# A Mamba layer and a LoRA feed-forward on eight cores: ScalarE's evacuations pulled forward, and the feed-forward in blocks of 512 tokens with streamed W2

## The reference, cut

```python
def _L0_attn_ref(x, ...):
    xz = jnp.einsum('bld,ed->ble', x, W_in)
    xc, z = jnp.split(xz, 2, axis=-1)          # xc: causal conv over 4 tokens, then silu
    ...
    xp = jnp.einsum('bld,ed->ble', xc, W_x)
    delta = jax.nn.softplus(xp[..., -1:] * w_dt + b_dt)
    dA = jnp.exp(delta[..., None] * A)
    dBx = (delta * xc)[..., None] * B_in[:, :, None, :]
    # h = dA_t * h + dBx_t ; y_t = sum_n h * C_t      (scan over the tokens)
    y = ys.transpose(1, 0, 2) + D_param * xc
    y = y * jax.nn.silu(z)
    return jnp.einsum('ble,de->bld', y, W_out)

def _L0_ffn_ref(x, W1, b1, W2, b2, scale):
    lt = jax.lax.dynamic_slice_in_dim(x, LORA_TOKEN_INDEX, LORA_DIM, axis=1)
    even = lt[:, ::2, :]; odd = lt[:, 1::2, :]
    m1 = (even[:, :4, :, None] * odd[:, :4, None, :]).reshape(Bx, Hx, Dx)
    m2 = (even[:, 4:, :, None] * odd[:, 4:, None, :]).reshape(Bx, Dx, Hx)
    h = x @ W1.T + scale * einsum(x, m1) + b1
    h = jax.nn.gelu(h, approximate=False)
    return h @ W2.T + scale * einsum(h, m2) + b2

x = _layernorm(x + _L0_attn_ref(x, ...))
x = _layernorm(x + _L0_ffn_ref(x, ...))
```

## Time and profile before

| | us |
|---|---|
| median of two runs | 8405.77 |
| profiled execution | 8392.8 |
| its slowest core (core 1), first to last instruction | 8391.2 |
| fastest core's span | 8322.1 |
| PE busy | 3725.1 (44%) |
| VectorE busy | 4821.4 (57%) |
| ScalarE busy | 3446.1 (41%) |
| GpSimd busy | 391.0 (5%) |

### The profile page before, as it was taken

The page is one execution under the profiler, slowest core; times in us unless marked ns, Lnnn a source line. Parts: engine busy times, 40 slices in busy tenths (PEclk is TensorE's granted clock), DMA queues, the critical chain, the costliest instruction groups (busy, mean ns, idle before and its releaser), DMA issues.

```text
span 8391.2 us, 72518 instructions; the slowest of 8 cores (8322.1 to 8391.2 us)
## 1 busy us (share of the span) xinstructions
PE 3725.1 (44%) x21344; PEld 2186.9 (26%) x21344; DVE 4821.4 (57%) x5521; ACT 3446.1 (41%) x8573; POOL 391.0 (5%) x522
## 2 busy tenths in 40 slices
PE   4446424234241433424243242433420078887888
PEld 2123313122130312313132131312210034444444
DVE  1000679797887979779797877969778500100010
ACT  4443545454454545445353454535434122222222
POOL 0010000000000000000000000000001000000000
PEclk9999657667675766766566675656765589888888
DMA  3676322223232222322223232222320310010000
GB/s 84 112 129 157 105 60 88 64 82 101 58 99 55 93 78 70 106 61 88 61 83 99 59 100 59 88 72 80 103 53 3 61 53 16 23 11 13 16 20 14
DMA packets 521966, 582.43 MB, mean 69 GB/s; under 512 B 413311, under 2 KB 413311, under 8 KB 482672
## 3 DMA queue, kind: packets, MB, share of 16 engines
q1 hardware_dynamic: 491408, 482.62, 18.9%
q0 software_dynamic: 30176, 95.17, 6.4%
HBM read 581.51 MB, written 71.84 MB: 78 GB/s over the span
## 4 chain that ended last, share of the span: by engine, by line
DVE 34%; DVEq 21%; PE 19%; DMA 6%; issue 5%; ACT 4%; another core or an unknown queue 1%; POOLq 1%; ACTq 0%; POOL 0%; SPq 0%
DVE hc L789 13%; DVEq L794 13%; PE ps_h L965 6%; PE ps_oB L993 6%; DMA wout_r<-woutT_scr 4%; DVE dbx L763 4%; DVE hc L807 4%; DVE hc L802 4%; DVEq L806 3%; DVEq L770 3%; PE ps_wo L380 2%; DVE hc L809 2%; DVE gtmp L815 1%; PE ps_h L968 1%; DVE hc L811 1%
## 5 line engine op out<-in xcount | busy, mean ns | idle before, releaser
L789 DVE TENSOR_TENSOR_SCAN hc<-dA,dbx 128x2048 bf16<-128x2048 f16 x512 | 2238.5, 4414 | 20.7 <-issue 2.3
L706 ACT ACTIVATE dA<-delta,a_sb 128x256 f16<-128x256 f32 x4096 | 1666.8, 494 | 431.9 <-DVE hc L789 428.0
L584 PE MATMUL ps_xz<-xT,w1s_r 128*128 128x256 bf16 x8192 | 1129.5, 305 | 522.5 <-ACT xc L659 391.9
L763 DVE TENSOR_TENSOR dbx<-vv,brep 128x2048 bf16<-128x2048 bf16 x512 | 607.4, 1228 | 867.6 <-ACT dA L706 651.2
L584 PEld LDWEIGHTS ps_xz<-xT,w1s_r 128*128 128x128 bf16 x8192 | 871.0, 109 | 751.4 <-issue 548.5
L600 PE MATMUL ps_xz<-xT,win_r 128*128 128x256 bf16 x2048 | 422.9, 389 | 1207.3 <-ACT zsil L667 1015.9
L380 PE MATMUL ps_wo<-wout_r,ybuf 128*128 128x512 bf16 x1024 | 332.3, 464 | 1322.8 <-DVE ybuf L819 1117.9
L802 DVE TENSOR_TENSOR hc<-hc,crep 128x2048 bf16<-128x2048 bf16 x512 | 612.8, 1238 | 20.1 <-issue 1.5
L600 PEld LDWEIGHTS ps_xz<-xT,win_r 128*128 128x128 bf16 x2048 | 263.6, 134 | 1361.1 <-issue 1262.8
L965 PE MATMUL ps_h<-y1T,w1t_sb 128*128 128x256 bf16 x4096 | 581.3, 289 | 18.3 <-DVE su_sb L1060 16.9
L706 ACT ACT_TABLE_LOAD x150 | 192.4, 1283 | 882.9 <-DVE hc L789 882.7
(11 more groups left out here) (116 smaller groups left out, 3990.3 us busy)
## 6 DMA issues: line engine op xcount, KB each, us to landing
w1s_r<-win1s_scr SPq DMA_DIRECT2D x256, 1024.0 KB, 5.0
win_r<-winT_scr SPq DMA_DIRECT2D x256, 256.0 KB, 2.9
wout_r<-woutT_scr SPq DMA_DIRECT2D x256, 256.0 KB, 2.6
win1s_scr<-p_stage SPq DMA_DIRECT2D x64, 256.0 KB, 2.3
brep<-bc_scr POOLq DMA_DIRECT2D x16, 1024.0 KB, 9.1
crep<-bc_scr POOLq DMA_DIRECT2D x16, 1024.0 KB, 13.4
out<-outsb SPq DMA_DIRECT2D x32, 512.0 KB, 3.2
p_wrow<-W_in POOLq DMA_DIRECT2D x48, 256.0 KB, 4.8
```

The costliest lines, as they stand in the source:

```text
L584: jx = t.matmul(pst[:], w1s_ring[jj % 2][:, (k4 * NKD + kt) * P:(k4 * NKD + kt + 1) * P], xT[par][:, kt * TE + 1 + k4:kt * TE + 1 + k4 + T ...
L706: jx = s.activation(da_t[:, n8 * T:(n8 + 1) * T], delta[dt % 8][:], AF.Exp, scale=a_sb[:, dt * NST + n:dt * NST + n + 1])
L763: jx = v.tensor_tensor(dbx[(jh0 + nh) % 4][:].rearrange("p (n t) -> p n t", n=8), vv[par][:, dt * T:(dt + 1) * T].unsqueeze(1) .broadcast_ ...
L789: jx = v.tensor_tensor_scan(hc[:, nh * 8 * T:(nh + 1) * 8 * T], dA[(jh0 + nh) % 4][:], dbx[(jh0 + nh) % 4][:], 0.0, OP.mult, OP.add)
```

## The change

Stage A: `prep_evac` for the next chunk runs in steps 4 to 10 (5, 5, 5, 5, 4, 4 and 4 of them) instead of 4 to 15, and `prep_xpev` at step 12 instead of behind step 15.

Stage B: blocks of TB = 512 tokens, 8 instead of 16. `w2t_sb` is gone; W2 comes in slabs of 128 x 1024 through four buffers `w2_r`, issued by SP, and is read twice a block (two passes of two token tiles each; four PSUM tiles are filled side by side, the loop over the slabs outside). h, u and t have 512 columns. There is one transposing PSUM tile instead of two, and one tile `ps_ut` for u and t. The layernorm's small steps all go to ScalarE (Ln and Exp in place of VectorE's reciprocal and ScalarE's root), tile by tile, with its scratch in `lnjB`. SP's stores of a block stand behind the block's last slab. y1cb is loaded 512 tokens at a time.

```diff
@@ stage A, ScalarE
                         if dt < 4:
                             for j2 in range(4 * dt, 4 * dt + 4):
                                 prep_trev(nxt, j2)
-                        else:
-                            n_ev = 3 if dt < 12 else 2
-                            m0 = 3 * (dt - 4) if dt < 12 else 24 + 2 * (dt - 12)
-                            for mm in range(m0, m0 + n_ev):
+                        elif dt <= 10:
+                            sched = [5, 5, 5, 5, 4, 4, 4]
+                            m0 = sum(sched[:dt - 4])
+                            for mm in range(m0, m0 + sched[dt - 4]):
                                 prep_evac(nxt, mm)
+                        if dt == 12:
+                            prep_xpev(nxt)
                 if nxt is not None:
-                    prep_xpev(nxt)
                     prep_delta_half(nxt, 0)
@@ stage B, tiles
-    w2t_sb = tsb2("w2t_sb", [P, NKH * DM], BF16)
-    y1cb = [tsb2(f"y1cb{j}", [P, 2 * DM], BF16) for j in range(2)]
+    w2_ring = [tsb2(f"w2_r{j}", [P, DM], BF16) for j in range(4)]
+    y1cb = [tsb2(f"y1cb{j}", [P, 4 * DM], BF16) for j in range(2)]
-    ps_trB = [stB.enter_context(nc.psum_tensor(f"ps_trB{j}", [P, P], BF16)) for j in range(2)]
-    ps_h = [stB.enter_context(nc.psum_tensor(f"ps_h{j}", [P, T], F32)) for j in range(2)]
-    ps_o = [stB.enter_context(nc.psum_tensor(f"ps_oB{j}", [P, 512], F32)) for j in range(2)]
+    lnjB = tsb2("lnjB", [P, DM], F32)
+    ps_trB = stB.enter_context(nc.psum_tensor("ps_trB", [P, P], BF16))
+    ps_h = [stB.enter_context(nc.psum_tensor(f"ps_h{j}", [P, TB], F32)) for j in range(2)]
+    ps_ut = stB.enter_context(nc.psum_tensor("ps_ut", [4, TB], F32))
+    ps_o = [stB.enter_context(nc.psum_tensor(f"ps_oB{j}", [P, 512], F32)) for j in range(4)]
@@ stage B, SP
-            i = sy.dma_start(out=w2t_sb[:].rearrange("p (k h) -> p k h", k=NKH),
-                             in_=w2T_scr.rearrange("k p h -> p k h"))
-            ev.inc(i, "hd", 16)
+            for i2 in range(nB):
+                if i2 > 0:
+                    emit_outst(i2 - 1)
+                for ps in range(2):
+                    for kt in range(NKH):
+                        jj = (i2 * 2 + ps) * NKH + kt
+                        if jj >= 4:
+                            ev.wait(sy, f"wo2K_{jj - 4}")
+                        j = sy.dma_start(out=w2_ring[jj % 4][:], in_=w2T_scr[kt])
+                        ev.inc(j, f"w2r{jj % 4}", 16)
+                        ev.mark(f"w2ld_{jj}", f"w2r{jj % 4}")
+            emit_outst(nB - 1)
@@ stage B, TensorE: transposes and output product
+                for j2 in range(32):
+                    if kc == 0 and j2 == 0:
+                        ev.wait(t, f"ltT_ev_{b}_{NKD - 1}")
+                    elif jj >= 1:
+                        ev.wait(t, f"y1T_ev_{(jj - 1) // 32}_{(jj - 1) % 32}")
+                    jx = t.transpose(ps_trB[:], ...
+                for ps in range(2):
+                    for kt in range(NKH):
+                        jj = (i2 * 2 + ps) * NKH + kt
+                        ev.wait(t, f"w2ld_{jj}")
+                        for gq in range(4):
+                            tM = ps * 2 + gq // 2
+                            nh = gq % 2
+                            if kt == 0:
+                                pj = i2 * 8 + ps * 4 + gq - 4
+                                if pj >= 0:
+                                    ev.wait(t, f"o2ev_{pj // 8}_{pj % 8}")
+                            jx = t.matmul(
+                                ps_o[gq][:],
+                                h_sb[:, kt * TB + tM * P:kt * TB + (tM + 1) * P],
+                                w2_ring[jj % 4][:, nh * 512:(nh + 1) * 512],
+                                start=(kt == 0), stop=False)
+                        ev.inc(jx, "pe", 1)
+                        ev.mark(f"wo2K_{jj}", "pe")
@@ stage B, ScalarE: layernorm, four tiles a block
+                for tM in range(4):
+                    sl = 8 * (tM % 2)
+                    ev.wait(s, f"y2add_{i2}_{tM}")
+                    if tM >= 2:
+                        ev.wait(s, f"outn_{i2}_{tM - 2}")
+                    dmp = lnjB[:]
+                    jx = s.activation(dmp, y2pre[tM % 2][:], AF.Square,
+                                      accum_out=c[:, sl + 0:sl + 1])
+                    s.drain()
+                    jx = s.activation(dmp, y2pre[tM % 2][:], AF.Copy,
+                                      accum_out=c[:, sl + 1:sl + 2])
+                    s.drain()
...
+                    s.activation(c[:, sl + 6:sl + 7], c[:, sl + 0:sl + 1],
+                                 AF.Ln, scale=1.0 / DM, bias=c[:, sl + 4:sl + 5])
+                    s.drain()
+                    jx = s.activation(c[:, sl + 7:sl + 8], c[:, sl + 6:sl + 7],
+                                      AF.Exp, scale=-0.5)
@@ stage B, VectorE: normalisation behind the adds
+                def emit_outn(tM):
+                    ev.wait(v, f"rstd2_{i2}_{tM}")
+                    if i2 * 4 + tM >= 2:
+                        pj = i2 * 4 + tM - 2
+                        ev.wait(v, f"outst_{pj // 4}_{pj % 4}")
...
+                    if nh == 1:
+                        ev.mark(f"y2add_{i2}_{tM}", "vc")
+                        if tM >= 1:
+                            emit_outn(tM - 1)
+                emit_outn(3)
```

More of the change, by code:

```diff
@@ L831, in build_nc @@
         return nc, ev.events
+    TB = 512
+    NCB = L // TB
+    nB = B_LOC * NCB
     stB = contextlib.ExitStack()
@@ L881, in _ @@
         def _(g):
-            for i in range(n_iters):
-                b, kc = it_bk(i)
-                par = i % 2
+            for i2 in range(nB):
+                b, kc = itB(i2)
+                par = i2 % 2
                 if kc == 0:
@@ new lines, in _ @@
+                    ev.wait(t, f"su2_{i2}_{plo}")
+                for ps in range(2):
+                    for kt in range(NKH):
+                        jj = (i2 * 2 + ps) * NKH + kt
[14 more added lines that the diff above has]
+                        ev.mark(f"wo2K_{jj}", "pe")
+                    for gq in range(4):
+                        tM = ps * 2 + gq // 2
+                        nh = gq % 2
+                        grp = ps * 4 + gq
+                        for plo in range(4):
+                            jx = t.matmul(ps_o[gq][:],
+                                          su2_sb[0:4, plo * TB + tM * P:plo * TB + (tM + 1) * P],
+                                          e2z[0:4, plo * DM + nh * 512:plo * DM + (nh + 1) * 512],
+                                          start=False, stop=False)
+                        jx = t.matmul(ps_o[gq][:], ones_sb[0:1, :],
+                                      b2_sb[0:1, nh * 512:(nh + 1) * 512],
+                                      start=False, stop=True)
+                        ev.inc(jx, "pe", 1)
+                        ev.mark(f"wo2_{i2}_{grp}", "pe")
@@ L1019, in _ @@
                     ev.mark(f"ltTev_{b}", "ac")
-                for j2 in range(16):
+                for j2 in range(32):
                     tt, dd = j2 // NKD, j2 % NKD
-                    ev.wait(s, f"y1T_tr_{i}_{j2}")
-                    jx = s.copy(y1T[par][:, dd * T + tt * P:dd * T + (tt + 1) * P],
-                                ps_trB[j2 % 2][:])
+                    ev.wait(s, f"y1T_tr_{i2}_{j2}")
+                    jx = s.copy(y1T[par][:, dd * TB + tt * P:dd * TB + (tt + 1) * P],
+                                ps_trB[:])
@@ L1025, in _ @@
                     jx = ev.inc(jx, "ac", 1)
[L1026 removed]
+                    ev.mark(f"y1T_ev_{i2}_{j2}", "ac")
                 for m in range(NMH):
                     pst = ps_h[m % 2]
[L1029 to L1032 removed]
+                    ev.wait(s, f"hpe_{i2}_{m}")
@@ L1033, in _ @@
+                    if i2 >= 1 and m == 0:
+                        ev.wait(s, f"wo2_{i2 - 1}_7")
+                    jx = s.activation(h_sb[:, m * TB:(m + 1) * TB], pst[:], AF.Gelu,
                                       bias=b1_sb[:, m:m + 1])
                     jx = ev.inc(jx, "ac", 1)
-                    ev.mark(f"hev_{i}_{m}", "ac")
-                for tM in range(2):
-                    ev.wait(s, f"y2add_{i}_1")
-                    ev.wait(s, f"y2add_{i}_{tM}")
-                    jx = s.activation(h_sb[:, 0:2 * DM].bitcast(F32), y2pre[tM][:], AF.Square,
-                                      accum_out=ln2col[:, 4 * tM + 0:4 * tM + 1])
+                    ev.mark(f"hev_{i2}_{m}", "ac")
@@ new lines, in _ @@
+                for grp in range(8):
+                    ps, gq = grp // 4, grp % 4
+                    tM = ps * 2 + gq // 2
+                    nh = gq % 2
+                    ev.wait(v, f"wo2_{i2}_{grp}")
+                    if grp >= 1:
+                        v.drain()
+                    if nh == 0 and (i2 > 0 or tM >= 2):
+                        pj = i2 * 4 + tM - 2
+                        ev.wait(v, f"ln2n_{pj // 4}_{pj % 4}")
```

(2 more changed lines are left out.)

218 lines of the change are left out of this document (77 added, 141 removed).

## The result

| | before | after |
|---|---|---|
| median, us | 8412.11 (42 runs) | 8455.17 (43 runs) |
| lowest and highest, us | 8362.51 to 8477.53 | 8410.68 to 8512.54 |
| profiled execution, us | 8392.8 | 8462.68 |
| its span on cores 1 and 5, us | 8391.2 and 8326.2 | 8459.7 and 8327.9 |
| its stage B on cores 1 and 5, us | 1730 and 1687 | 1757 and 1706 |

The ratio is 1.0049, 95% interval 1.0036 to 1.0062: the change makes the kernel half a per cent slower. Forecast were 8345 us, 0.8% faster; the time lies inside the range of 8255 to 8540, on the wrong side of the old one. Stage B (here always from the issue of w1's load to the end of the span) was to get 91 us shorter before the clock's share. It got 19 us longer on core 5 and 27 on core 1.

A forecast was written before the change was run, and what follows sets the result against it. VectorE was taken to bound stage A and TensorE stage B. From the profiled 8392.8 us, -91 for stage B, +15 for stage A and +20 for the clock gave 8337, a median near 8345; range 8255 to 8540.

The forecast's parts named there:

- Output product, +38 forecast: Stage B: w2 slabs through four buffers, 2.97 us from release to use, pace 0.96 us a slab; +38 us.
- the slabs set the pace: Stage B rival: eight cores streaming slow landings to 4.1 us, 1.35 a slab, +173 us, 8520 in all; chance 0.13.
- h product, -115 forecast: Stage B: 512-column matmuls at 221 ns replace 256-column ones at 132 ns; 646 us becomes 530, -115.
- t products, -27 forecast: Stage B: 11.0 us a block instead of 7.15 a chunk, 88 us for 114; -27.
- the load: Start of stage B: only w1 is awaited instead of both weights, doubled y1cb load included; -20 us.
- transposes with one tile: Stage B: one PSUM tile instead of two, 0.77 us a transpose, 196 us for 98; +98.
- u: Stage B's low-rank product: 5.0 us a block, 40 us for 46; -6.
- the batch change: Stage B: PE's wait for y1cb, now 1 MB instead of 0.5, beside w2's first slabs; +10 us.
- The gap: Layernorm gap before stage B's transposes: 6.5 us a block, bounds 5 and 9, 52 us for 121; -69.
- Stage A, +15 forecast: Evacuations pulled forward put ScalarE on the edge at step 8; 1 us a chunk, +15, bounds 0 to 75.
- the copy's move, costed at 0: Stage A: B/C copy moved to step 12 gains nothing, hidden in 759.4 us that ScalarE stands anyway; 0.
- Clock, +20 forecast: Stage B: lower granted clock because PE is dense for 131 of 184 us instead of 73 of 97; +20 us.

The follow-up runs named there:

- e10: The changed kernel with eight w2 buffers instead of four and nothing else; 8394.2 us for 8483.96 of the kernel before, ratio 0.9866.
- e11: e5 with the 20 low-row matmuls behind each pass replaced by 128-row ones, low-rank part and bias of the output omitted; 8252.91 us for 8483.96.
- e4: New stage B with the old stage A, without the 256 rank-4 matmuls of the h product; 8377.22 us, one run.
- e3: New stage B with the old stage A, transposes alternating between two PSUM tiles instead of one; 8393.39 us for 8465.36, ratio 0.996.
- e8: e1 with only half of each w1s slab loaded after the first two; 8372.69 us, one run.
- e7: Kernel before with only stage A changed: four evacuations in each of steps 4 to 11, B/C copy at step 13; 8390.48 us for 8390.36.
- e12: e7 with the B/C copy left behind step 15, as in the kernel before; 8471.97 us for 8527.03, one run each.
- e1: Stage A of the changed kernel with stage B of the kernel before; 8437.23 us for 8465.36, ratio 1.001.
- e9: Stage A of e7 combined with stage B of e5; 8286.59 us for 8483.96 of the kernel before, ratio 0.9821.
- e6: e5 with each pass's 20 low-row matmuls spread four at a time behind slabs 4, 9, 14, 19 and 24; 8277.79 us for 8390.36, ratio 0.9864.
- e5: Old stage A, new stage B with two transpose tiles and eight w2 buffers instead of four; 8248.73 us for 8390.36, ratio 0.9827.

## Why the prediction was wrong

Two terms of stage B were too fast, by 92 and 27 us. Together they are more than the 91 that the stage was to gain, and so the sign turned.

- **Output product, +38 forecast, +130 measured.** The step that failed is the slab's 0.96 us: it was 1.106, just above the 1.1 named as the point from which the gain is gone. From release to use the slab needed 3.55 us and not 2.97; w2's landings had a median of 3.0 to 3.1 us where stage A's had 2.6, and the rest lies outside the landing. The 2.97 (2.95 by its own terms) was worked out from SP's issues in the projection, a stage with another load on the queues, and then divided by four buffers as if no slab were ever later than the mean. e10 puts the price at 109 us on core 5. The rival "the slabs set the pace", given 0.13, named this place and the right direction, landings slower under eight cores' streams, and put them at 4.1 us and 1.35 a slab, too much. It was latency over too few buffers and not bandwidth: eight buffers stream at 268 GB/s without a wait. The rest of the 130 is a balance. The prediction cost a tail by its count of matmuls and put the clock in one lump of +20 elsewhere; that the clock falls over 20 low-row matmuls stood in no term. e11 measured it at 22 to 25. Against it stand 48 fewer changes between 128 rows and 4 (16 tails for 64), by e4's 0.2 us an estimated 10.
- **h product, -115 forecast, -88 measured.** The step that failed reads 132 ns a matmul of 256 columns and 221 of 512 out of two groups of different make. The first divided 1.19 us by nine, and 0.2 of the 1.19 is the change of rows around the rank-4 matmul, once a group whatever the columns; e4 shows it. With it a group of 512 is 2.15 and not 1.994, which is 40 us over 256 groups. Against that stood 12 us: starts at the half clock were put at 2.5 a block, 20 in all, and came to 8 (558.3 less 256x2.15).
- The Trainium skill ("TensorE: Matmul & The Clock Gate", Back-to-back issue gap) was set aside there, with the 109 and 216 ns of its N/2.4+2.5. The new traces agree with that formula: 128 matmuls in 27.8 us are 217 ns. The page calls it the gap of an isolated matmul and gives some 131 ns for a stream of 512 columns, which no run here shows. By the formula alone h would still gain nothing, and it gained 88: 256x(2x1.19-2.15)=59 by one rank-4 matmul with its changes of rows for two, and 29 by fewer starts at the half clock (in the old kernel 646.6 less 16x32x1.19, 37 us, for 8).
- **t products, -27 forecast, -20 measured**: 11.8 us a block for 11.0; a group repeats every 2.88 us, not every 1.77+0.97.
- **Right in size**: the load (-24 for -20), transposes with one tile at 0.767 us (e3: 94 us for 98), u, the batch change (+9 for +10). The gap was 5.7 us and not 6.5 (30.2 a block less 32x0.767), within its bounds.
- **Stage A, +15 forecast.** The mechanism was right, that five evacuations a step put ScalarE on the edge at step 8 and that late slabs go through; e8 removed the lateness with the slabs' second halves, e7 by spacing the work. Two sizes were off. On cores at the full clock the waits are 4 to 33 us, but the copy's move, costed at 0 because ScalarE and GpSimd stand anyway, gave back 14 (e12 against e7). That step failed; what the copy held up at the chunk's end is open. In the changed kernel's profile cores 0 to 3, with 584 to 933 us of stage A at 0.81, waited 46 to 66 us and began stage B 35 late. Whether the low clock did it isn't shown: in e10 cores 0 to 3, with 786 to 942 us of it, waited 20 to 50. The bounds of 0 to 75 hold all of it.
- **Clock, +20 forecast.** On core 1, stage B took 43 us more than on core 5 before and 51 after, with 294 and 365 us of it at 0.81. So at most 8 are the change's, and the longer stretch alone would explain them. Nothing here ties the 0.81 to the change. In stage B of e1 cores 2 and 3 stood at 0.81 for 735 and 690 us and cores 0 and 1, under the same load, for none; in e9 it was cores 6 and 7, and not 4 and 5. The Trainium skill ("TensorE: Matmul & The Clock Gate", the peak-current limiter in The HAM clock gate) has the whole die of four cores at 13/16 once three of them run dense matmuls; these runs disagree.

On the profiled execution the working gave 8337 and 8462.68 came out. Of the 126 between them, 118 are stage B on core 1 (+27 for -91), less the 20 for the clock, and 26 are stage A (+41 for +15); the other 2 are rounding and lie outside the core's span. (The forecast's last step was off as well: 8337 and 13 are 8350, not 8345.)

## What to carry to other kernels

Before a resident operand is replaced by a stream, take the time from a buffer's release to the next use under the new load, divide it by the time of one slab, add one for the slab in use, and have at least as many buffers. Here that is 3.55/0.87 and one, 5.1: four buffers of 256 KB cost 109 us on core 5 and eight cost none; five, six and seven weren't run. Never divide a group's time by its matmuls when one of them has another shape: read the fixed part from two group sizes first. And a schedule that is free at the mean can have lost its slack: ask for each pulled-forward step what happens when its load is late or the clock low, since an even spacing of the same work cost at most 2 us in either case (e7, e12).

## What the hardware showed

- A change between matmuls of 128 rows and of 4 or 1 costs about 0.1 us each way, at 256 columns as at 512: 0.2 us a group of h at 256 and at 512 columns; in e6 twenty full matmuls and four low ones repeat every 5.38 us, 24x0.2165 and 0.18.
- Twenty matmuls of four rows and one row let the granted clock fall to 1.2 GHz while TensorE is busy without a gap; the same twenty with 128 rows don't (e5 and e11). It fell in every first pass's tail of e5's cores 4 to 7 and in 4 of 32 second ones. The tails of five in the kernel before kept 1.00 on cores 4 to 7.
- A granted clock of 0.81 comes pair by pair of neighbouring cores, not die by die, and costs the old stage B some 110 us when it holds for 735 us of it (e1, cores 0 and 2).
